# The second stage of a two-stage image kernel: drive products in three couples, the first and last pair by GpSimd, and the rows of B and C stored amid the preceding unit's spreads

## What is computed

```python
xz = x @ in_w.T;  xi, z = split(xz)
xc = silu(causal_conv4(xi) + conv_b)                 # 128 inner channels
dt_raw, B, C = split(xc @ xproj_w.T, [4, 4 + 16])    # 16 states
dt = softplus(dt_raw @ dt_w.T + dt_b)
for t in steps:
    h = exp(dt_t * A) * h + dt_t * x_t * B_t         # h: 128 channels x 16 states
    y_t = sum over states of h * C_t
out = (y + xc * D) * silu(z) @ out_w.T
```

## Time and profile before

| | |
|---|---|
| runs of the kernel before | 3948.23, 3955.54, 3961.82 us (median 3955.54) |
| span of the profiled execution | 3947.8 us |
| of it stage 2 | from about 693 us on, 128 units |
| VectorE busy | 3749.1 us |
| TensorE busy | 3654.2 us |
| GpSimd busy | 3277.5 us |
| ScalarE busy | 2937.3 us |
| share of the 16 DMA engines, 2100 to 3900 us | 0.88 |

### The profile page before, as it was taken

How to read it: one execution, slowest core, us unless ns; L and a number is a source line. 1 busy time by engine, 2 the same in 40 slices (tenths; PEclk the granted TensorE clock), 3 DMA queues, 4 the chain that set the end, 5 groups by cost and what they waited for, 6 DMA issues and landing times. The chain is left out here.

```text
span 3947.8 us, 34409 instructions
## 1 busy us (share of the span) xinstructions
PE 3654.2 (93%) x8780; PEld 1519.6 (38%) x8780; DVE 3749.1 (95%) x3409; ACT 2937.3 (74%) x4422; POOL 3277.5 (83%) x1542
## 2 busy tenths in 40 slices
PE   7999999899999999999999999999999999999998
PEld 3444444333333333333333333333333333333333
DVE  7778787999999999999999999999999999999998
ACT  3454554787888878888888888878888888878785
POOL 2221222899999999999999999999999999999998
PEclk9999999999999999999999999999999999999999
DMA  4142324888888888898888888888899888988886
GB/s 113 33 130 58 109 74 149 325 344 338 347 348 348 344 345 340 345 350 353 347 342 350 347 347 342 352 347 341 343 353 349 339 346 347 350 340 344 336 348 264
DMA packets 203157, 1181.06 MB, mean 299 GB/s; under 512 B 30960, under 2 KB 31760, under 8 KB 68816
## 3 DMA queue, kind: packets, MB, share of 16 engines
q1 hardware_dynamic: 200128, 1177.64, 77.5%
q10 hardware_dynamic: 2832, 1.23, 0.1%
HBM read 1144.03 MB, written 34.73 MB: 299 GB/s over the span
## 5 line engine op out<-in xcount | busy, mean ns | idle before, releaser
L1537 POOL TENSOR_TENSOR read<-state,bc_all 128x1024 f32<-128x1024 f32 x1024 | 2398.9, 2360 | 117.0 <-DVE state L1601 88.0
L1601 DVE TENSOR_TENSOR_SCAN state<-decays,p_drive 128x1024 f32<-128x1024 f32 x1024 | 2297.9, 2274 | 33.0 <-ACT p_drive L1436 9.8
L1306 PE MATMUL p_y<-read,ident 128*128 128x512 f32 x4096 | 1921.9, 602 | 14.0 <-POOL read L1537 13.9
L1428 ACT ACTIVATE decays<-dt,wa 128x496 f32<-128x496 f32 x2048 | 1337.2, 703 | 121.1 <-DVE state L1601 118.5
L1306 PEld LDWEIGHTS p_y<-read,ident 128*128 128x128 f32 x4096 | 764.9, 191 | 990.6 <-issue 833.2
L1588 DVE TENSOR_TENSOR p_drive<-bc_all,p_dtx 128x1024 f32<-128x1024 f32 x768 | 906.5, 1210 | 0.0
L1554 POOL TENSOR_TENSOR pool_drive<-dtx,bc_all 128x1024 f32<-128x1024 f32 x256 | 602.4, 2353 | 12.2 <-DMA bc_all<-bc_scratch 11.9
L766 POOL TENSOR_TENSOR pad<-map_all,xc 128x512 f32<-128x512 f32 x96 | 138.9, 1476 | 519.1 <-DMA map_all<-map_scratch 498.3
L1436 ACT COPY p_drive<-pool_drive 128x1024 f32<-128x1024 f32 x256 | 260.8, 1019 | 270.8 <-DVE state L1601 270.8
L1302 PE MATMUL p_y<-xconv,d_diag 128*128 128x512 f32 x256 | 144.6, 647 | 202.0 <-DVE gated L1611 202.0
L556 PE MATMUL p_conv<-pad,wm 128*128 128x512 f32 x576 | 267.5, 600 | 1.8 <-issue 1.8
(11 more groups left out here) (162 smaller groups left out, 3214.1 us busy)
## 6 DMA issues: line engine op xcount, KB each, us to landing
bc_all<-bc_scratch SPq DMA_DIRECT2D x1024, 1024.0 KB, 7.3
map_all<-map_scratch SPq DMA_DIRECT2D x48, 512.0 KB, 5.7
norm_rows<-xn SPq DMA_DIRECT2D x32, 280.0 KB, 5.8
norm_in<-norm_rows SPq DMA_DIRECT2D x64, 140.0 KB, 6.6
norm_in<-norm_rows SPq DMA_DIRECT2D x64, 139.8 KB, 7.6
fresh<-in_x SPq DMA_DIRECT2D x32, 256.0 KB, 6.8
x<-in_x SPq DMA_DIRECT2D x32, 256.0 KB, 3.6
mid_x<-x SPq DMA_DIRECT2D x32, 256.0 KB, 6.5
```

The costliest lines, as they stand in the source:

```text
L1306: nc.tensor.matmul(p_y[:], ident[:], read[:, s % DEEP, :], start=False, stop=(s == N - 1)).then_inc(y_added, 1)
L1428: nc.scalar.activation(decays[:, s % DEEP, :].rearrange("p (q t) -> p q t", t=SIDE)[:, :, 1:], dt[b][:, :, 1:], ACT.Exp, scale=wa[m][:, s: ...
L1537: nc.gpsimd.tensor_tensor(read[:, s % DEEP:s % DEEP + 2, :], state[:, s % DEEP:s % DEEP + 2, :], bc_all[s // CHUNK][:, :, 1, :], ALU.mult) ...
L1601: nc.vector.tensor_tensor_scan(state[:, at:at + 2, :].rearrange("p s n -> p (s n)"), decays[:, at:at + 2, :].rearrange("p s n -> p (s n)") ...
```

## The change

Three things are altered in stage 2, and no arithmetic. The two pairs whose drive GpSimd makes become 0 and 7 (`BY_POOL = (0, 14)`). As `make_drive` is called six steps ahead and `move_drive` two, GpSimd's product for the second of them goes from step 2 to step 8, and ScalarE's move from step 6 to step 12. VectorE's order becomes: scan 0, drives 1 and 2, scan 1, gate, scan 2, drives 3 and 4, scans 3 and 4, drives 5 and 6, scans 5, 6 and 7. And SyncE issues the stores of unit u + 1 behind the fourth spread of unit u, after a wait for chunks 4 to 7 of unit u - 1 to have landed (it read the same scratch), and waits for their landing only before the first spread of u + 1.

```diff
-    BY_POOL = (0, 8)
+    BY_POOL = (0, 14)
@@ store_rows
         for j in two:
             sp.dma_start(bc_scratch[b][:, j, :], ...).then_inc(rows_stored, 16)
+
+    def rows_landed(sp, u):
+
         sp.wait_ge(rows_stored, 32 * u + 32)
@@ spread_first
         store_rows(sp, 0)
+        rows_landed(sp, 0)
@@ sync_program
+        store_rows(sp, 1)
         for u in range(1, UNITS):
-            store_rows(sp, u)
+            rows_landed(sp, u)
             for k in range(CHUNKS):
                 spread_chunk(sp, u, k)
+                if k == CHUNKS // 2 - 1 and u + 1 < UNITS:
+
+                    for late in range(k + 1, CHUNKS):
+                        sp.wait_ge(bc_loaded[late], 16 * u)
+                    store_rows(sp, u + 1)
@@ vector_program, slot
-            for half in two:
-                p = 4 * half
+            scan_pair(u, 0)
+            if u == 0:
+                last_norm(dve, 1)
+            for p in (1, 3, 5):
+                make_drives(u, p)
+                if u == 0 and p == 1:
+                    last_norm(dve, 2)
+                make_drives(u, p + 1)
                 scan_pair(u, p)
-                if u == 0 and half == 0:
-                    last_norm(dve, 1)
-                make_drives(u, p + 1)
-                if u == 0 and half == 0:
-                    last_norm(dve, 2)
-                make_drives(u, p + 2)
+                if p == 1:
+                    if u == 0:
+                        last_norm(dve, 3)
+                    if before:
+                        apply_gate(u - 1, 1 - b, before)
                 scan_pair(u, p + 1)
-                if u == 0 and half == 0:
-                    last_norm(dve, 3)
-                if half == 0 and before:
-                    apply_gate(u - 1, 1 - b, before)
-                scan_pair(u, p + 2)
-                make_drives(u, p + 3)
-                scan_pair(u, p + 3)
+            scan_pair(u, 7)
```

## The result

| | before | changed |
|---|---|---|
| median of the runs, us | 3951.9 | 4202.9 |
| ratio, 95% interval | | 1.0629 (1.0611 to 1.0648) |
| span of the profiled execution, us | 3947.8 | 4200.7 |
| a unit, us | 25.19, seven of 26.6, mean 25.3 | 26.3 or 28.0, mean 27.3 |
| mean granted clock of TensorE | 0.993 | 0.966 |

A forecast was written before the change was run, and what follows sets the result against it. VectorE, 95% busy, set the pace at 25.19 us a unit; the new order's loop through GpSimd takes 25.79. The 0.60 more in about 126 units adds 76 to 3955.5: 4031.5 us, 1.9% slower, range 3980 to 4075.

The forecast's parts named there:

- VectorE's floor: VectorE's own work in the new order, no product alone and no exposed waits: 24.82 us a unit.
- The loop through GpSimd: From S3 through GpSimd's R3 to R7, TensorE's adds and the next gate back to S3: 25.79 us a unit.
- R3: GpSimd's fourth read in a unit, which needs S3; taken at 2.32 us.
- S3: VectorE's fourth scan of a unit's eight, counted from 0; taken at 2.28 us.
- from the end of R7 to the gate, with TensorE free: 2.08: Term of the loop through GpSimd: TensorE's four passes after the last read, 2.08 us, read from the last unit.
- R7: GpSimd's eighth and last read in a unit; taken at 2.36 us, before TensorE's adds and the gate.
- R5: GpSimd's sixth read in a unit; taken at 2.32 us.
- 0.3 more: Extra TensorE time if R7 finds it still summing the next unit's dt: unit of 26.1 us, +115 us in all.
- the clock: Rival, 12%: TensorE's four passes behind R7 run at the lower clock, 1.7 us longer in one unit of four, 4082 us.
- The loop through ScalarE: From S5, VectorE's sixth scan, through ScalarE's two moves and the work between to the next unit's first scan: 25.57 us.
- The rows of B and C: SyncE's earlier stores of these rows and later wait for their landing: no gain and no cost, 0.
- VectorE's pace: Rival, 12%: GpSimd and ScalarE hold nothing up, the unit is 24.82 us and the kernel takes 3909 us.

The follow-up runs named there:

- the filler: Changed kernel plus two unused matrix products (four passes) a unit on TensorE, before the adds of pair 5: 4081.9 us, 1.0331 to the kernel before.
- the fastest version: Changed kernel with pair 7's drive product at step 6, half the sum of dt behind pair 7's adds, ScalarE's steps reordered: 3924.9 us, 0.9923.
- the late sum of dt: Changed kernel with TensorE's sum of the next unit's dt moved behind the adds of pair 7: 4048.0 us, 1.0245 to the kernel before.

## Why the prediction was wrong, point by point

- **VectorE's floor**: right. Three couples of 2.24 us, no exposed wait, and 24.83 in one unit of four of the version in which nearly nothing else binds.
- **The loop through GpSimd**: right as a mechanism, with GpSimd's wait before R3 (0.84 measured; 14.3 less 13.4 forecast) and S3 as its anchor. Its term "from the end of R7 to the gate, with TensorE free: 2.08" is the step that failed, twice.
- First, TensorE isn't free. I took the 2.08 from the last unit, the only one without a sum of dt for a successor. In the others R7 ends at 2039.96 and the gate starts at 2042.58, 2.62 later, because 16 passes stand behind R5. That the passes behind R5 are a chain of their own I priced at "0.3 more" and left out of the sum; it is 0.54 (26.33 with these passes, 25.79 without), some 68 us in 126 units.
- Second, **the clock**. I had it as a rival at 12%, with the right price for one fall (1.7 us; the two kinds of unit differ by 28.01 - 26.33 = 1.68), but at the passes behind R7 and in one unit of four, and argued against it that TensorE idles less at the gate. The price fits by luck of the place: it is the price of any four slow passes on the path. (The rival's 4082 is also added up wrongly: 4031.5 + 54 is 4085.5.) I looked for idle time only where it had been before. The delay of R5 makes a new gap ahead of the adds of pair 5, 2.0 to 2.5 us long, where the kernel before had 0.04 on average and at most 0.42 in the units I had looked at, and the falls come right behind it, in 73 of 128 units. With the filler they don't come, and 121 us go.
- The sum by these terms: 76 + 68 + 72 x 1.67 = 264 us; the spans differ by 252.9. Nearly all of the rest is in the kernel before: it had seven units of 26.6 us in place of 25.19, 10 us in all, which the changed kernel doesn't have; 264 - 10 = 254. These seven are the clock too: in each it fell some 8.7 us into the unit, behind 1.9 us of idle at the gate. The five scans that had waited for the move stand behind five of these falls.
- **The loop through ScalarE**: right in mechanism and size (25.57 forecast, 25.51 when it binds), and right that it doesn't add.
- **The rows of B and C**: right, 0.
- **The rivals**: VectorE's pace was not reached. The edit does take a wait away from VectorE, and the time rose all the same (1.063); with the loops shortened it fell (0.992). The Trainium skill, Perfetto Trace Analysis, section Identifying the Most-Contended Engine, says to optimize the engine with the highest occupancy first. By that rule the time should have fallen: this case doesn't agree for the change as it was made, and does for the fastest version.
- **The range**: its upper end was the lower part of one missing term alone. I had two terms whose prices were in the text (0.3 and 1.7 us a unit, at that place) and no case in which both held.

## What to carry to other kernels

When an instruction is moved on one engine without changing any engine's total, look for the loops that cross a unit's border (producer, consumer, the engine behind it, and back by a buffer or a gate), and sum each by rows, on every engine along it, in the unit that has both neighbours, not in the last one. Put a movable instruction where its engine waits anyway: here two steps were worth 5% of the time. And for TensorE ask where the new order opens a gap, not whether the old gap shrinks: four useless passes in it were worth 3%.

## What the runs showed of the chip that I had not expected

- The clock fell behind idle stretches of only 2.0 to 2.5 us, though not behind each. In the changed kernel, in successive units, 2.51 us of idle was followed by full clock, 2.03 by the low one, 1.98 by full, 2.45 by low. Over the whole trace it fell behind 40 of 60 gaps of 2.5 us and 31 of 61 of 2.0, and from the third unit on two units at full clock never follow each other. The length of the one gap doesn't decide it. With 1.2 us at that place (product at step 6) the clock over the whole execution was 0.995, with 0.3 to 0.8 (the filler) 0.997, with the gap 0.966. With the late sum of dt, gaps of 1.4 to 2.1 left it at 0.988. In the kernel before it fell behind 7 of 26 gaps of 1.9 us at the gate. What else decides was not tried.
- A transfer that is waited for by 0.8 us a unit can set the pace of the whole loop: product at step 4, 1.0663, where the 7.4 us from the last read of a chunk's buffer to the first use of its new content are part of the unit of 27.3.
